# Four transformer layers on one core: the third layer's queries, keys and mask turned by whole transposes, padded one-hot tables, fewer shift transfers, a refitted step order

## The reference

```python
x = x + tanh(g_xattn[0]) * L0_xattn(ln(x), ctx, ctx, adj, mask)     # 16 heads of 8, bias + mask
x = x + tanh(g_ffn[0])   * L0_ffn(ln(x))       # argmax over 8 experts, 128x128 each
x = x + tanh(g_xattn[1]) * L1_xattn(ln(x), ctx, ctx)                # 16 heads, rms, rotary, causal
x = x + tanh(g_ffn[1])   * L1_ffn(ln(x))       # top 2 of 8 low-rank experts on a shared MLP
x = x + tanh(g_xattn[2]) * L2_xattn(ln(x), ctx, key_mask)           # 4 query heads of 32, one key head
x = x + tanh(g_ffn[2])   * L2_ffn(ln(x))       # argmax over 8 experts, 128x512 each, gelu
x = x + tanh(g_xattn[3]) * L3_xattn(ln(x), ctx, ctx)                # 16 heads of 8
x = x + tanh(g_ffn[3])   * L3_ffn(ln(x))       # reaches only the first 512 tokens (two rows)
```

```python
q = rope(rmsnorm(x) @ q_w) * 32**-0.5            # 4 heads
k = rope(rmsnorm(ctx) @ k_w); v = rmsnorm(ctx) @ v_w   # one head
logits = q @ k.T
masked = where(key_mask, logits, -2.3819763e+38)
out = softmax(masked) @ v @ out_w
```

## Time and profile before

| | |
|---|---|
| time, median of 3 runs | 1016.82 us (1016.78 to 1017.49) |
| the profiled execution's own time | 1021.1 us |
| its span, first to last instruction | 1019.3 us |
| mean granted TensorE clock | 0.913 of full |
| busy | PE 897.2 us (88%), DVE 750.6 (74%), ACT 512.7 (50%), POOL 304.5 (30%) |
| chain that ended last | PE 58%, DVE 26%, ACT 7%, issue 6%, POOL 1%, DMA 1% |

### The profile page before, as it was taken

How to read it: one execution, slowest core, us unless ns; L and a number is a source line. 1 busy time by engine, 2 the same in 40 slices (tenths; PEclk the granted TensorE clock), 3 DMA queues, 4 the chain that set the end, 5 groups by cost and what they waited for, 6 DMA issues and landing times.

```text
span 1019.3 us, 19907 instructions
## 1 busy us (share of the span) xinstructions
PE 897.2 (88%) x7572; PEld 599.6 (59%) x7572; DVE 750.6 (74%) x1849; ACT 512.7 (50%) x813; POOL 304.5 (30%) x324
## 2 busy tenths in 40 slices
PE   3688778889899999998999779789888899999997
PEld 3443456545676777874476334475456676887644
DVE  6799989888657444678838999989785757458671
ACT  2582644455442434326886656544645344433666
POOL 4512056454342301110144021654634332101100
PEclk8898978799897989997999998987999899999979
DMA  9100000000000000000001000000000000000000
GB/s 322 50 2 2 2 1 1 1 4 2 1 1 2 1 2 1 2 7 7 28 28 42 3 2 2 1 1 2 3 3 1 1 1 2 2 1 2 2 7 17
DMA packets 11743, 14.29 MB, mean 14 GB/s; under 512 B 1604, under 2 KB 10716, under 8 KB 11396
## 3 DMA queue, kind: packets, MB, share of 16 engines
q1 hardware_dynamic: 11552, 12.88, 3.9%
q10 hardware_dynamic: 100, 0.14, 0.1%
HBM read 11.55 MB, written 1.05 MB: 12 GB/s over the span
## 4 chain that ended last, share of the span: by engine, by line
PE 58%; DVE 26%; ACT 7%; issue 6%; POOL 1%; DMA 1%; ACTq 0%; DVEq 0%
PE banks L1056 52%; DVE nm_row L1529 6%; DVE probs L1548 3%; PE banks L744 3%; ACT probs L1005 3%; DVE xn_row L1484 1%; PE banks L1110 1%; DVE st_row L1372 1%; DVE mv_row L1374 1%; ACT qT_row L922 1%; DVE wide L1617 1%; PE banks L1127 1%; DMA probs<-in_small 1%; DVE qr_row L726 1%; ACT wide L1035 1%
## 5 line engine op out<-in xcount | busy, mean ns | idle before, releaser
L1529 DVE TENSOR_REDUCE nm_row<-banks 128x4 f32<-128x1024 f32 (+1 forms) x192 | 209.4, 1125 | 19.1 <-PE banks L1056 18.1
L1005 ACT ACTIVATE probs<-banks 128x1024 f32<-128x1024 f32 (+1 forms) x144 | 128.3, 929 | 45.3 <-PE banks L1056 44.6
L838 POOL TENSOR_TENSOR rstd_row<-rstd_row,neghalf 128x2 f32<-128x2 f32 x66 | 47.7, 722 | 306.9 <-DVE rstd_row L1479 242.3
L1056 PE MATMUL banks<-probs,vpad 128*32 128x256 f32 (+1 forms) x1536 | 107.1, 400 | 14.6 <-ACT probs L1000 11.9
L1056 PE MATMUL banks<-wide,c 128*128 128x256 f32 x512 | 119.1, 386 | 0.0
L1056 PE MATMUL banks<-kT_row,qT_row 48*128 48x256 bf16 (+2 forms) x896 | 93.2, 298 | 14.5 <-ACT probs L1005 5.8
L1056 PEld LDWEIGHTS banks<-wide,c 128*128 128x128 f32 x512 | 94.6, 190 | 15.7 <-issue 0.6
L1056 PE MATMUL banks<-qT_row,kT_row 50*128 50x256 bf16 (+2 forms) x896 | 88.9, 298 | 16.6 <-ACT probs L1005 6.8
L1000 ACT ACTIVATE probs<-probs 128x1024 f32<-128x1024 f32 x64 | 67.2, 1054 | 54.0 <-DVE probs L1548 52.6
L1056 PEld LDWEIGHTS banks<-kT_row,qT_row 48*128 48x128 bf16 (+1 forms) x896 | 37.7, 111 | 73.9 <-issue 52.0
L838 POOL TENSOR_TENSOR kss_row<-kss_row,neghalf 128x32 f32<-128x32 f32 x8 | 44.4, 5544 | 122.7 <-DVE kss_row L728 122.7
(11 more groups left out here) (226 smaller groups left out, 1647.7 us busy)
## 6 DMA issues: line engine op xcount, KB each, us to landing
c<-in_c SPq DMA_DIRECT2D x1, 2500.0 KB
wide<-in_mask SPq DMA_DIRECT2D x8, 256.0 KB, 2.8
qT_row<-mT_row SPq DMA_DIRECT2D x96, 4.0 KB
c<-in_c SPq DMA_DIRECT2D x1, 1194.5 KB
xn_row<-in_ctx SPq DMA_DIRECT2D x8, 128.0 KB, 3.8
x_row<-in_x SPq DMA_DIRECT2D x8, 128.0 KB, 2.6
late<-in_late SPq DMA_DIRECT2D x2, 512.0 KB, 14.9
out<-x_row SPq DMA_DIRECT2D x8, 128.0 KB, 1.9
```

Of the source, the lines that this page charges most:

```text
L838: return pool.tensor_tensor(t, t, neghalf[:, 0:n], ALU.pow)
L1005: act.activation(dst[:, :, 0:w], src[:, :, 0:w], ACT.Exp, scale=1.0 if l == 2 else HD ** -0.5).then_inc(sem["probs"], 1)
L1056: return pe.matmul(dst, lhsT, rhs, start=start, stop=stop, **kw)
L1529: V.tensor_reduce(nm[b][:, t, :, 2 * jp:2 * jp + 2], ps[:, :, :, 0:kn], AX.X, ALU.max, negate=True).then_inc(sem["max"], 1)
```

## The change

The third layer's queries are rotated by DVE straight into a 128x512 table (`q2`, now in the buffer `biasT`) with each head at the start of a 64-column block; POOL has zeroed it before and set a column of ones behind each head. A head pair is then 128 columns wide, and `q_flip` is four transposes of 128x128. The keys are written twice into a 128x256 table (`k2`) by one DVE instruction with a repeated source, together with the mask's fill value in one column and a one in another, and `k_flip` is two transposes of 128x128. ACT copies each result whole. The mask's bytes come once for all rows, by one transfer (`mrow8`, a strided view of 128x16 single bytes), which is queued ahead of the large constants; they become fill values in `fold`.

`ohT`, `selb`, `pickb` and `small_parts` have 128 partitions, zeroed by POOL at the start below what they hold, and the products read all of them. The shift goes out in two transfers of two rows each, in the third layer in one. The planner's costs, its classes of array use, `LEAD` and `FAVOUR` are new; `SAME` is zero and has no effect.

```diff
-        "k_flip": [("PE", .44), ("ACT", .91)], ("k_flip", 2): [("PE", .99), ("ACT", .65)],
+        "k_flip": [("PE", .44), ("ACT", .91)], ("k_flip", 2): [("PE", .24), ("ACT", .27)],
-        "q_flip": [("PE", .44), ("ACT", .91)], ("q_flip", 2): [("PE", 2.09), ("ACT", 1.07)],
+        "q_flip": [("PE", .44), ("ACT", .91)], ("q_flip", 2): [("PE", .49), ("ACT", .49)],
-LANDS = {"consts": CONSTS, "load": 4, "mask": 4, "fetch": 4, "shift_flip": 3.4, "store": 2}
+LANDS = {"consts": CONSTS, "load": 4, "mask": 4, "fetch": 4, "shift_flip": 2.1, "store": 2}
...
+                        sp.dma_start(mrow8[:, :].rearrange("p (b t) -> p b t", t=NT), dram["mrow"].rearrange("b (t p) -> p b t", p=P), allow_slow_non_contiguous=True).then_inc(const_in, 16)
                         for n in LATE_PACKS:
...
-                        for r in range(2):
-                            sp.dma_start(mrow8[b][STK * r + MD:STK * r + MD + 1, :], dram["mrow"][row:row + 1]).then_inc(sem["row_in", b], 16)
...
-                            for r in range(2):
-                                for part in range(2):
-                                    at_row = STK * r + KD + part
-                                    n = 16 * r + 8 * part
-                                    sp.dma_start(qT[b][at_row:at_row + 1, :, :], mT[b][n:n + 8, :]).then_inc(sem["shift_in", b], 16)
+                            for part in range(2):
+                                at_row = KD + part
+                                sp.dma_start(qT[b][at_row:at_row + STK + 1:STK, :, :], mT[b][16 * part:16 * part + 16, :]).then_inc(sem["shift_in", b], 16)
...
-                            ch.link(pool.memset(q2T[b][MD:MD + 2, :, :], 1.0))
-                            pool.memset(q2T[b][STK + MD:STK + MD + 2, :, :], 1.0).then_inc(sem["q_ones"], 1)
+                            ch.link(pool.memset(q2[b][:, :, :], 0.0))
+                            pool.memset(q2[b][:, :, :].rearrange("p t (h c) -> p t h c", h=MQ)[:, :, :, MD:MD + 1], 1.0).then_inc(sem["q_ones"], 1)
...
                             for t in range(NT):
-                                pe.transpose(bank("kT_ps", s)[0:MD, t * P:(t + 1) * P], k2[b][:, t, :], ident)
-                                ins = mm(bank("kT_ps", s)[STK:STK + MD, t * P:(t + 1) * P], k2[b][:, t, :], ident)
+                                ins = pe.transpose(bank("kT_ps", s)[:, t * P:(t + 1) * P], k2[b][:, t, :], ident)
...
-                                    pe.transpose(bank("qT_ps", s)[0:MD, cols], q2[b][:, t, hh, :], ident)
-                                    ins = mm(bank("qT_ps", s)[STK:STK + MD, cols], q2[b][:, t, 2 + hh, :], ident)
+                                    ins = pe.transpose(bank("qT_ps", s)[:, cols], q2[b][:, t, hh * P:(hh + 1) * P], ident)
...
-                            mm(dst, biases("b1_f2")[:, ft * P:(ft + 1) * P], ohT[b][0:3 * E, :], stop=False)
+                            mm(dst, biases("b1_f2")[:, ft * P:(ft + 1) * P], ohT[b][:, :], stop=False)
...
-                            half_turn(dve, ch, kk[:, :, None, :], kr[b][:, :, 0:MD].unsqueeze(2), k2[b][:, :, None, :], "ck2", "sk2", 1).then_inc(sem["k_rot"], 1)
...
-                                ch.mark(V.memset(k2T[b][STK * r + MD:STK * r + MD + 2, :], 1.0))
...
-                                ins = V.tensor_scalar(k2T[b][one, :], mrow8[b][one, :], 0.0, FILL, ALU.is_equal, ALU.mult)
...
+                            ch.mark(V.tensor_copy(k4[:, :, :, MD:MD + 1], mfill[:, row, :, None, None].to_broadcast([P, NT, 2, 1])))
+                            half_turn(dve, ch, kk[:, :, None, :], kr[b][:, :, None, 0:MD], kr[b][:, :, None, MD:2 * MD], k4[:, :, :, 0:MD],
+                                      "ck2", "sk2", 1).then_inc(sem["k_rot"], 1)
```

More of the change, by code:

```diff
@@ L130 @@
 AHEAD = 2
-LEAD = [[277.4, 280.3, 275.9, 278.4, 283.5, 1082.8, 306.8, -285.0],
[7 rows of a table removed]
[L139 to L146, removed]
+LEAD = [[279.5, 281.2, 278.7, 279.6, 318.6, 1300.3, 259.4, 176.7],
[7 rows of a table added]
+SAME = 0.0
+FAVOUR = {"again": 138.3, "bias": 29.3, "choose": 9.0, "consts": 13.4, "deep": -60.4, "deep_out": -18.6, "divide": 68.0, "expand": -5.3, "fetch": 6.1,
+          "finish": -140.3, "flip": 20.9, "fold": 150.1, "fore": 96.2, "gate": 140.9, "inner": -0.5, "k_flip": 3.1, "k_low": 4.8, "k_mid": -56.6,
+          "k_turn": 34.2, "kv": 32.0, "lift": -145.5, "load": -39.8, "mask": 186.8, "max": -0.6, "mix": -0.8, "norm": 3.2, "num_flip": -1.3, "o_flip": 64.1,
+          "outer": -0.1, "plus": -29.7, "q_low": 56.7, "q_mid": 9.9, "q_turn": 5.1, "query": 1.1, "route": 145.3, "shift": 43.3, "shift_flip": 8.5,
+          "split": 0.4, "spread": 2.7, "stats": 12.9, "store": 25.7, "sums_flip": 0.3, "weigh": -1.7}
+COST = {"load": [("SP", .4), ("PE", .27), ("ACT", .27), ("DVE", 1.56), ("POOL", .67)], "mask": [("SP", .4)], "fetch": [("SP", .6)], "consts": [("SP", 3)],
         "split": [("ACT", 1.25), ("DVE", 4.6)], "fold": [("ACT", .37), ("DVE", 1.75), ("PE", 0), ("POOL", 0)],
@@ L206, in array @@
         return "halves", "halves"
-    if kind in ("weigh", "shift_flip") or (kind == "choose" and l != 1) or (kind in ("k_flip", "q_flip") and l == 2):
+    if kind in ("weigh", "shift_flip") or (kind == "choose" and l != 1):
         return "strips", "strips"
@@ L212, in array @@
         return "sides", "sides"
[L213 to L216, removed]
     return "whole", "whole"
@@ L254, in starts_after @@
                 "q_flip": [(of("query", 2), "DVE") if l == 2 else (of("q_low", l), "DVE")],
-                "max": [(of("q_flip", l, last), "ACT"), (of("k_flip", l, last), "ACT")] + ([(of("bias", 0), "POOL")] if l == 0 else [(of("plus", 2), "POOL")] if l == 2 else []),
+                "max": [(of("q_flip", l, last), "ACT"), (of("k_flip", l, last), "ACT")] + ([(of("bias", 0), "POOL")] if l == 0 else []),
                 "shift_flip": [(of("shift", l), "DVE")],
@@ L273, in starts_after @@
                 "norm": [(of("stats", l), "POOL")],
+                "query": [(of("plus", 2), "POOL")] if l == 2 else [],
                 "o_flip": [(of("num_flip", l), "ACT")] if l != 2 else [],
@@ L761, in half_turn @@
                 ch.link(V.tensor_tensor(tmp[:, :, :, H2:MD], f[:, :, :, 0:H2], sn[:, :, None, H2:MD].to_broadcast(shape), ALU.mult))
-                return V.tensor_tensor(dst, dst, tmp, ALU.add)
+                copies = list(out.shape)
+                return V.tensor_tensor(out, dst.to_broadcast(copies), tmp.to_broadcast(copies), ALU.add)
             @block.sync
@@ L820, in _ @@
                 pool.memset(spreads[:, :], 0.0).then_inc(setup_zero, 1)
+                pool.memset(selb[:, :], 0.0)
+                pool.memset(pickb[:, :], 0.0)
+                pool.memset(small_parts[:, :], 0.0).then_inc(setup_zero, 1)
+                for b in range(ROWS):
+                    filled = pool.memset(ohT[b][:, :], 0.0)
                 pool.memset(neghalf[:, :], -0.5)
@@ L958, in _ @@
                     if kind == "k_flip" and l == 2:
-                        act.wait_ge(sem["kT_ps"], at("kT_ps", s))
-                        for r in range(2):
-                            rows = slice(STK * r, STK * r + MD)
-                            ins = act.activation(k2T[b][rows, :], bank("kT_ps", s)[rows, 0:SEQ], ACT.Copy)
-                        ins.then_inc(sem["kT"], 1)
+                        evac(k2T[b], "kT_ps", bank("kT_ps", s)[:, 0:SEQ], "kT")
                     if kind == "flip":
@@ L970, in _ @@
                     if kind == "q_flip" and l == 2:
[L971 to L976 removed]
+                        evac(q2T[b], "qT_ps", bank("qT_ps", s)[:, :].rearrange("p (h q) -> p h q", h=2), "qT")
                     if kind == "shift_flip":
```

102 lines of the change are left out of this document (49 added, 53 removed), and 14 rows, old and new, of the table LEAD.

## The result

| | before | after |
|---|---|---|
| median, us (four runs each) | 1017.15 | 985.02 |
| lowest and highest, us | 1016.78, 1018.15 | 981.34, 987.0 |
| profiled execution and span, us | 1021.1, 1019.3 | 987.0, 985.3 |
| mean granted clock in it | 0.913 | 0.912 |

The ratio is 0.966, with a 95% interval of 0.9621 to 0.9699: faster by 32 us, where 21 were forecast.

A forecast was written before the change was run, and what follows sets the result against it. TensorE, busy 897.2 of 1019.3 us, was taken as the bound. Late stages -21.2 (85% of 24.9), DVE-full stages -1.0, start +1: total -21.2, or 2.08% off the median, 996 us; range 982 to 1009.

The forecast's parts named there:

- Transposes: Third layer's `q_flip` and `k_flip` as whole transposes: -19.8 us of TensorE over eight rows, 85% of it to arrive.
- One-hot tables: Padded bias, `pick` and `spread` products avoid array-mode edges, 0.14 us a group: -4.5, -2.2 and -1.7 us of TensorE.
- padding itself is free: Products over 128 rows instead of 8 cost nothing extra; bounds -0.01 and +0.1 us each.
- VectorE and ACT: Fewer small DVE steps, -0.6 to -1.0 us a row, and one ACT copy instead of two: counted as nothing.
- Shift: Two transfers fewer let `attend` begin 1.27 us earlier after each wide `shift_flip`: counted 0, up to -4 us.
- Order: Rows keep their order and steps shift by a few places: 0, bounds -6 to +8 us.
- Start: Single-byte mask transfer ahead of the constants delays constants and masks: +1 us, bounds 0 to +5.
- The first: Rival: freed TensorE time turns into waiting on DVE, ACT and row chains; 40% arrives, -10, 1007 us; chance 0.18.
- The second: Rival: all 28 us arrive, shorter shift adds 4, one or two clock falls go; -33, 984 us; chance 0.18.
- The third: Rival: new order opens TensorE gaps at layer changes, five more clock falls cost 17 us; -4, 1013 us; chance 0.11.
- The fourth: Rival: single bytes clog the queues at the start, transfer over 30 us; +8, 1025 us; chance 0.06.
- The gain was to lie from 250 to 460 us and after 800: Sign in the later profile: gain in these stretches, the first 230 us nearly as long as before.

The follow-up runs named there:

- e2: Kernel before with the new planner's numbers, so all old instructions in the new order: 1038.57 us, ratio 1.0153 to before.
- set 1: First of three sets of follow-up runs, each with the kernel before run beside them; that kernel's median there was 1025.46 us.
- e8: Changed kernel with four small DVE settings after each third-layer key rotation, on a spare tile, and ACT copying queries and keys in halves: 994.89 us.
- f2: e1 with ACT's two half copies and DVE's four small settings a row put back: 1004.28 us.
- f1: e1 with each shift in four transfers again: 982.08 us.
- e6: Changed kernel with each shift in four transfers again: 995.12 us.
- e1: Changed kernel with the planner's numbers of before, so new instructions in the order of before: 983.18 us.
- a0: The changed kernel run once more, nothing altered: 984.67 us, ratio 0.9599 to before.
- e3: Changed kernel with new planner costs but LEAD and FAVOUR of before, a third order: 1017.59 us.
- e7: Changed kernel with the single-byte mask transfer made four times, ahead of the constants: 990.56 us.
- e5: Changed kernel with each whole third-layer query and key transpose split into a transpose and a 32-bit product of 64 columns: 1003.1 us.

## Why the prediction was right, and where it was not

The mechanism held for the two terms that carry the sum: fewer microseconds of TensorE where TensorE is full. Four terms undone one at a time in the new order give 18.4 + 14.2 + 10.4 + 10.2 = 53.2 us; all of them undone (e2) give 53.9. With some 5 us of scatter on each term this closeness is in part luck.

So is the forecast's. It had 16.8 + 5.4 + 0 + 0 = 22.2 us for these four, 31 too few, and two thirds of what it missed lay in the two terms that it put at nothing (VectorE with ACT, and the shift). It came out only 11 off because 13 of the 53.9 only make good what the new order does to the old instructions (1038.57 - 1025.46), and because the kernel before stood 8 us lower in the first runs than in set 1.

**Transposes**: 19.8 us at 85%, so 16.8; measured 18.4. Right in size, and the 85% was about right.

**One-hot tables**: counted 4.5 + 2.2 + 1.7 = 8.4, of which 5.4 were to arrive; measured 14.2 and 17.2. This is a term of the sum that was mis-sized. The step that failed is "0.225 each", with "so leaving costs 0.06" behind it. That 0.225 was the mean of twelve passes that hold 0.11 of the way in; the pitch is 3.45 / 16 = 0.216. By groups before and after, the edges are 0.20 to 0.30 us in the third layer, by what follows, and 0.14 to 0.23 in the first, not 0.14. The 32 groups of the third layer take 3.80 us on average before and 3.59 after, the first layer's at full clock and without a gap 2.10 and 1.92: 32 x 0.21 + 16 x 0.18 = 9.6 us. The 24 `spread` steps have theirs (in after, eight `spread` products take 0.88 instead of 0.98, two of the second layer 0.22 instead of 0.32), some 2 us more. That leaves 2 of the 14.2 without a place.

The Trainium skill says that a change of tiling mode drains TensorE ("TensorEngine Tiling (Array Packing)", Key Properties). The traces agree in kind, with 0.20 us for going in and 0.10 for leaving at full clock.

That padding itself is free was right: 0.12 us for a product of 128 rows.

**VectorE and ACT**: "I count nothing", from a window with 20 us of 50 to spare; measured 10.2, and 21.1 in the other order. This was a failed step of reasoning. The window averages 250 to 300 us; the instructions stand at 233.6 us in the first row, where DVE was busy for 18.90 of the 25 us from 225 to 250, and, more to the point, ahead of a row's norm in an in-order queue. Their 1.1 us a row goes onto that row's chain. How the 10 and 21 divide between DVE and ACT was not tried, and the steps of e8 and f2 are stand-ins (1.45 us a row linked together, where 1.1 went and a part of that came back), not the instructions of before.

**Shift**: "I count 0, with up to -4". In the order of before it is 0 (f1), in the new one -10.4 (e6). The planner's `LANDS` fits this: the new order places `attend` for a landing 1.3 us earlier.

**Order**: 0, and it is 0 for the new instructions (e1 against a0: 1.5 us, inside the spread). But it is not one term beside others, as the sum had it. It costs 13 us with the old instructions in set 1 (1038.57 - 1025.46), and 33 with leads and costs that don't match (e3), which is more than the bound of +8.

**Start**: +1; about 2 by e7, if the first transfer costs what the three added ones do on average. The price of 0.055 us a packet was too high for these: 2.3 us for 2064 packets on 16 engines are 0.018. In the window 10 to 15 us the queues were 0.67 busy and moved 157 GB/s, where before they were 0.99 busy at 341. POOL's wait for row 3's mask grew to 3.93 us from 3.14, and `sgn` on ACT came at 36.64, earlier than 38.54. POOL and ACT of after:

```profile
29.67 1.94 POOL L857 TENSOR_SCALAR wide<-wide 128x512 f32<-128x512 int32 x1 [3.93 <-DMA wide<-in_mask]
```

```profile
36.64 0.20 ACT L939 ACTIVATE sgn<-c 128x8 f32<-128x8 f32 x1
```

**The rivals.** The first (waiting, 1007) is out: TensorE is at 49 of 50 in the last stages. Between 250 and 300 us it is at 43.85, which is the 44 that this rival named, but the stage is not as long as before: the third layer's first product comes 7 us earlier. The second has the number, 984, but not the grounds: it had all 28 us arrive, 4 of the shift and 4 to 7 of the clock, and the clock's mean didn't change (0.913 and 0.912). What filled its place are the edges, the shift in the new order, and the small steps of DVE and ACT. The third is out for this order, and e3 shows that it was a real danger. The fourth is out: 2.3 us for the transfer, where it needed over 30. The gain was to lie from 250 to 460 us and after 800. By the phases of bias products it is 17 us up to the end of the third layer's first half (454.5 to 437.2), 5 from there to 703 us, and 15 behind, of which the tail gives back 3.

Two things stay open. In the order of before, undoing DVE and ACT costs 21.1, the tables 17.2 and the shift nothing, together 38; the whole change is worth 34 to 42 there, so the transposes would be left with next to nothing. Undoing them alone in that order was not tried, and the parts may simply not add up.

And e1 runs at a granted clock of 0.932 to 0.937 in 983 to 987 us, a0 at 0.912 to 0.915 in 984 to 986 (its fourth run at 0.930 in 977). The traces say where. TensorE's bias products in e1:

```profile
L1056 PE MATMUL banks<-ohT_row,small_parts x32: 269/273/283, 327.8 to 912.7; 128*128 128x256 bf16 x32
L1056 PE MATMUL banks<-small_parts,ohT_row x16: 216/219/230, 133.4 to 672.5; 128*128 128x128 bf16 x16
```

and two windows of it, with the columns of the earlier trace rows:

```profile
130.00:230.00 100.00, 79.30 (x812) 54.26 (x806) 89.31 (x227) 51.45 (x80) 57.35 (x35) 0.93 0.01 2
230.00:330.00 100.00, 91.73 (x797) 67.67 (x798) 73.16 (x239) 47.42 (x105) 40.65 (x62) 0.98 0.01 2
```

From 130 to 230 us its clock is 0.93, where after has 0.83 and before 0.82, and from 230 to 330 us 0.98 for 0.93 and 0.88. The third layer's first product comes at 327.8, 12.6 us ahead of after; the first layer's last is 8.1 ahead, the third layer's last 0.4. So the order of before wins with the new instructions early, in part by the clock, and loses it again in the second group of rows. A part of what the change is worth in that order is therefore clock and not removed work, and how much was not measured. No version beat the changed kernel by more than the runs scatter.

## What to carry to other kernels

Read a pitch from rows that begin after the transition, and price both edges of a group; 0.1 to 0.2 us an edge, over 48 groups and 24 `spread` steps, is some 12 us, and undoing it cost 14 to 17. An engine's average slack over 50 us doesn't make its instructions free: ask what stands behind them in its queue and who waits for that. A hand-fitted order is fitted to durations, so judge a change of instructions and its order together, in both orders where that can be had.

## What the runs showed of the hardware

- A 32-bit turn in two halves, a transpose and a two-pass product of 64 columns each, takes 0.585 us (e5), one of 32 columns each 0.54, and a whole transpose of 128 columns 0.13 (half of the earlier trace rows).
- Single bytes go out as one packet each: 2064 packets for a transfer of 2048 of them (e7).
- SP issues a transfer of 2048 single bytes in 0.39 us, a second one directly behind it in 1.42, and the third and fourth in 2.3 to 2.4, which is probably the time that the queues need for one.
- A transfer that writes two rows of a table is cheaper to issue than one that writes one: 0.495 for 0.635 us.
- The changed kernel's time follows the mean clock it was granted: 977.02 us at 0.930, 981.34 at 0.926 and 984 to 987 at 0.912 to 0.922. The kernel before ranged from 1015.27 to 1029.21 us, its four medians from 1017.15 to 1025.46. The 2 us named in the prediction as the limit of what can be told were too few; 5 would be fair between medians of different sets.
